# Two jobs of one unit moved ahead on TensorE: the GRU products to the second step, the sums over the table to the third, in a graph layer with a GRU update

## The reference

```python
h = relu(layernorm(x))
xs, xd = h[src], h[dst]
att = sigmoid(xs @ W_att[:d] + xd @ W_att[d:] + b_att)
messages = (xs @ W_msg + b_msg) * att
aggregated = segment_sum(messages, dst)
gi, gh = aggregated @ W_ih.T + b_ih, h @ W_hh.T + b_hh
r = sigmoid(i_r + h_r); z = sigmoid(i_z + h_z); n = tanh(i_n + r * h_n)
h_new = (1 - z) * n + z * h
out = x + gamma * (h_new - mean) * rsqrt(var + 1e-5) + beta
```

## Time and profile before

| what | value |
|---|---|
| median of 3 runs | 2257.42 us (2254.52 to 2258.43) |
| profiled execution, its own time | 2257.88 us |
| its span in the profile | 2256.1 us |
| busy share PE / DVE / ACT / POOL | 91% / 89% / 88% / 74% |
| mean granted clock of PE | 0.965 of full |

### The profile page before, as it was taken

One profiled execution on the slowest core, in us unless ns is written; L12 is line 12 of the kernel. 1 busy time (PEld: TensorE's weight loads), 2 busy tenths in 40 slices (PEclk: granted clock), 3 DMA queues, 4 the chain that ended last, 5 costly groups with the idle time before them and its releaser, 6 DMA issues.

```text
span 2256.1 us, 53903 instructions
## 1 busy us (share of the span) xinstructions
PE 2055.7 (91%) x18202; PEld 1994.3 (88%) x18202; DVE 2012.9 (89%) x4413; ACT 1996.3 (88%) x6980; POOL 1660.4 (74%) x1578
## 2 busy tenths in 40 slices
PE   3536999999999999999999999999999999999997
PEld 3525999999999999999999999999999999999996
DVE  5967899999999999999999999999999999999974
ACT  1368999999999999999999999999999999999943
POOL 4575777777777777777777777777777777777760
PEclk8865999999999999999999999999999999999998
DMA  6862222222222222222222222222222222222236
GB/s 164 237 172 62 56 60 62 59 60 60 62 62 62 63 58 64 61 63 59 63 59 62 59 61 60 63 60 62 60 61 63 59 62 60 61 61 64 58 108 231
DMA packets 167473, 171.57 MB, mean 76 GB/s; under 512 B 79462, under 2 KB 131736, under 8 KB 166944
## 3 DMA queue, kind: packets, MB, share of 16 engines
q0 software_dynamic: 49856, 102.96, 20.3%
q1 hardware_dynamic: 114564, 61.63, 10.5%
q10 hardware_dynamic: 2776, 3.52, 0.7%
HBM read 141.32 MB, written 26.65 MB: 74 GB/s over the span
## 4 chain that ended last, share of the span: by engine, by line
ACT 53%; PE 23%; DVE 14%; issue 7%; DMA 2%; SPq 1%; POOL 0%; ACTq 0%; DVEq 0%
ACT big L901 41%; PE ps L1456 12%; ACT gate_ring L897 9%; DVE big L1200 4%; PE ps L1441 4%; PE ps L1451 3%; DVE gate_ring L1184 2%; DVE key_hot L1170 1%; PE ps L1462 1%; PE ps L1463 1%; DVE lo_hot L1163 1%; DMA big<-in_x_dram 1%; DVE big L1129 1%; DMA row_ring<-node_table,set_idx 1%; ACT n_blk L906 1%
## 5 line engine op out<-in xcount | busy, mean ns | idle before, releaser
L773 POOL DMA_INDIRECT row_ring<-node_table,set_idx x1480 | 1571.8, 1062 | 473.4 <-issue 334.5
L901 ACT ACTIVATE big<-set_score,big 128x128 f32<-128x128 f32 x5096 | 1633.2, 394 | 81.0 <-PE ps L1456 80.7
L1456 PE MATMUL ps<-big 128*128 128x128 f32 x10192 | 1447.4, 281 | 0.0
L1456 PEld LDWEIGHTS ps<-big 128*128 128x128 f32 x10192 | 1265.0, 193 | 0.0
L1200 DVE TENSOR_TENSOR big<-ps,big 128x784 f32<-128x784 f32 x832 | 802.0, 964 | 10.2 <-ACT big L901 5.4
L1441 PE MATMUL ps<-gate_ring,row_ring 128*128 128x64 f32 x2960 | 534.8, 263 | 78.0 <-DVE gate_ring L1184 72.7
L1441 PEld LDWEIGHTS ps<-gate_ring,row_ring 128*128 128x128 f32 x2960 | 454.0, 194 | 124.4 <-DVE gate_ring L1184 110.7
L1184 DVE SCALAR_TENSOR_TENSOR gate_ring<-lane,set_rel,gate_ring 128x64 f32<-128x64 f32 x1480 | 412.9, 279 | 140.1 <-ACT gate_ring L897 135.0
L897 ACT ACTIVATE gate_ring<-set_win,row_ring 128x64 f32<-128x64 f32 x1480 | 493.2, 341 | 30.5 <-DMA row_ring<-node_table,set_idx 27.3
L1451 PE MATMUL ps<-key_hot,lo_hot 128*128 128x196 bf16 x3328 | 425.8, 250 | 14.4 <-DVE key_hot L1170 9.5
L1170 DVE TENSOR_TENSOR key_hot<-lane_key,set_key 128x1568 bf16<-128x1568 bf16 x416 | 402.0, 966 | 0.0
(11 more groups left out here) (129 smaller groups left out, 917.2 us busy)
## 6 DMA issues: line engine op xcount, KB each, us to landing
row_ring<-node_table,set_idx POOLq DMA_INDIRECT x1480
big<-in_x_dram SPq DMA_DIRECT2D x48, 256.0 KB, 5.6
h_blk<-hT_spill SPq DMA_DIRECT2D x97, 64.0 KB
node_table<-big SPq DMA_DIRECT2D x24, 258.0 KB
hT_spill<-big SPq DMA_DIRECT2D x24, 256.0 KB, 4.8
out_dram<-big SPq DMA_DIRECT2D x24, 256.0 KB
set_win<-dst_scores SPq DMA_DIRECT2D x148, 32.0 KB
set_score<-dst_scores SPq DMA_DIRECT2D x52, 64.0 KB
```

Of the source, the lines that this page charges most:

```text
L773: nc.gpsimd.indirect_dma_start(row_ring[:, t % ROWS_RING, :], None, table, bass.IndirectOffsetOnAxis(ap=set_idx[:, t // SET % 2, t % SET:t ...
L901: return nc.scalar.activation(a_buf[b % 2][:, h, :], set_score[:, b % 2, :], ACT.Sigmoid, bias=m_all[:, h, D:ROW])
L1456: return nc.tensor.matmul(ps[:, AM_BANK, 0:P], m_all[:, h, 0:D], a_buf[b % 2][:, h, :], start=h == 0, stop=h == HI - 1)
```

## The change

Three things change, all on PE. The sums over the table start at step 2 instead of 3. The GRU products of the finished block stand in step 1 instead of 2. In step 2 the `build` comes behind the part of the sums and not ahead of it. No instruction is added or taken away, and no other engine's program differs.

```diff
-PARTS_AT = 3
+PARTS_AT = 2
 DENSE_AT = 7
 GROUP_LAG = 3
-GRU_AT = (2, 10, 18, 26, 33)
+GRU_AT = (1, 10, 18, 26, 33)
...
-                    if u < BLOCKS and s % PER_BEAT in (0, 2):
+                    builds = u < BLOCKS and s % PER_BEAT in (0, 2)
+                    if builds and s != PARTS_AT:
                         build(u, 2 * (s // PER_BEAT) + (s % PER_BEAT) // 2)
                     if u and s == PARTS_AT:
                         pe.wait_ge(pairs_kept, u * (2 * BEATS))
...
                         last.then_inc(block_parts, 1)
+                    if builds and s == PARTS_AT:
+                        build(u, 2 * (s // PER_BEAT) + (s % PER_BEAT) // 2)
                     k = job_at(u, s, GRU_AT)
```

## The result

| | before | changed |
|---|---|---|
| median of 12 runs each | 2258.29 us (2254.52 to 2261.99) | 2263.99 us (2261.38 to 2266.70) |
| span of the profiled execution | 2256.1 us | 2262.1 us |

The ratio is 1.0021, with a 95% interval of 1.0013 to 1.0028. The change makes the kernel slower by 0.2%, where 24 us less were forecast; the range ended at 2257.

What follows compares the result with a forecast made beforehand. The prediction took two equally long chains, POOL's gathers and the loop of ACT, DVE and PE, to bound the kernel. Its sum was 2257.9 − 21.5 − 2.2 − 0.7 = 2233.5 us, range 2206 to 2257.

Steps and rivals of the forecast that it cites:

- What bounds the kernel: Main loop: POOL's gathers, never idle, and the loop of ACT, DVE and PE run equally long, 38.62 us a unit.
- The loop's 1.17 us: Start of each unit: ACT's wait for the sums falls from 1.47 to 0.3 us, shortening the loop by 1.17.
- PE's idle time: Step 1 on PE: the GRU products fill the idle 0.75 us before the next tile, which is then gone.
- What 1.17 us is worth: POOL's gathers limit the gain: from 1.367 to 1.351 us each, −21.5 us over 1345 gathers.
- rival 2: POOL keeps 1.367 us a gather and the loop's gain turns into ACT's waits for gathers: 2255 us, chance 0.22.
- The ends: First units: POOL's stops at the ring may go, −2.2 us; last unit: part of the sums done earlier, −0.7.
- rival 3: Builders always meet gathers at a bad moment, POOL slower, from a mean of 1.372 on: 2289 us, chance 0.09.
- Rival 1: The loop alone bounds the kernel, POOL settling at 37.45 us a unit: 2199 us, up to 2210, chance 0.20.
- The Trainium skill: Its rule that `tensor_tensor` does not hinder gather descriptors would give POOL 1.25 us a gather in a shorter unit.

Runs made afterwards that it cites:

- e1: The kernel before with every eighth gather left out from tile 40 on: 2257.57 us, 0.9984 of the kernel before.
- e2: The changed kernel with every eighth gather left out from tile 40 on: 2222.46 us, 0.9831 of the kernel before.
- e7: The changed kernel with the key builder cut into two instructions of half the size: 2228.19 us, 0.9868 of the kernel before.
- e9: The kernel before, PE's old order, with the key builder cut into two instructions: 2255.26 us, 1.0000 of the kernel before.
- e10: e7 with ACT's first gates of a unit's first GRU job in step 9 instead of 8: 2212.53 us, 0.9809 of the kernel before.
- e5: The changed kernel without the key builder (L1170) from unit 1 on, old patterns in its place: 2199.28 us, one execution.
- e6: The changed kernel without the other builder (L1163) from unit 1 on, old patterns in its place: 2212.24 us, one execution.
- e3: The kernel before with only the GRU products moved to step 1, sums still from step 3: 2266.88 us, 1.0026 of the kernel before.

## Why the prediction was wrong

**What bounds the kernel** was right: two chains of equal length, one of them POOL's without a pause. e1, e2, e7 and e9 show both halves of it. That the change would shorten the loop was right too.

**The loop's 1.17 us.** ACT's wait for the sums went from 1.47 us a unit to 0.07 (3.2 us in 46 units). Worked out was 0.3. But the loop gains less than that: with fewer gathers the new order brings 35 us (e2 against e1), 0.70 a unit, where 58 were worked out for the loop alone. The step missed a wait: ACT's first GRU gates stand in step 8 and need DVE's last step of the job before, in step 5; ACT now reaches them too early. With fewer gathers this wait is 28.9 us in e2 (0.6 a unit), and where it is removed, in e10, the kernel gains 13 us more than e7, each against its own kernel before. In the kernel before it does not show in the main loop, presumably because the wait ahead of it hid it. The forecast did not hang on this size, since it had POOL set the time either way.

PE's idle time did not go either. Over the main loop PE waited before for the masks of gathered tiles by

```profile
PE ps L1441 <- DVE gate_ring L1184: 49.6, 84, 1.1
```

and it waits 47.0 us with the change (in the waits above). Of the 49.6, 38.3 stood ahead of the tile of step 2; of the 47.0, 24.0 stand ahead of that of step 1 and 10.1 ahead of that of step 17.

**What 1.17 us is worth: here it failed.** The step took 1.351 us a gather, the middle between 1.367 and the 1.335 of four units with a broken pattern. Measured: 1.371. Of the forecast −21.5 us came +6.0 over the same 1345 gathers. Those four units were picked because their pattern was broken, and that says little about the new pattern. DVE ran the key builder 8 times in two of them and 7 times in the other two, against 8 in a unit on average, so the number of builders explains little. They differ in how long the gathers are that meet it: 1068, 1108 and 1103 ns on average in the three fast ones, 1394 in the slow one, 1225 over all 46 units. That depends on the moment of the meeting, which nothing in the step could foretell, and it came out at 1244. The honest figure was the mean of all 46, and rival 2 with 2255 was worked out from it. That the builders are what makes gathers long was right (e5, e6). That their cost is per unit of work, and not per time, no run separates.

**The ends.** Gathers 40 to 134: −2.8 for the −2.2 forecast. After the last gather: −2.1 for −0.7.

**The rivals.** The result lies between rival 2, unchanged pitch, and rival 3, slower. The mechanism is rival 3's at a small size: ACT does follow right behind the gathers, and the builders meet them at worse moments. The pitch came out at 1.371, where rival 3 began to count from 1.372, and its 2289 was far too much. The medians differ by 5.7 us, and 6.0 come from the pitch in the one pair of profiles; the rest of the balance there (5.0 ahead of gather 10, −2.8 and −2.1) is partly the scatter between executions. Rival 1, the loop alone at 2199, is what the kernel goes towards when gathers are fewer or cheaper: 2222 in e2, 2228 in e7, both with POOL waiting for the ring.

**The Trainium skill.** By "SBUF — State Buffer", "Who interferes with whom", a `tensor_tensor` should not hold up the descriptors of a gather, which the page marks as inferred. The same section of the Trainium skill also says that a `tensor_tensor` with both inputs in SBUF contends with GpSimd's reads, which the prediction left out. e5 and e6 show that both builders, `tensor_tensor` on bf16 from SBUF to SBUF, make gathers longer: by 97 and 38 ns of the mean. The measurement decides: the inference does not hold for this pair, and it was no reason to count on rival 1. Whether it is a read of POOL that is held up, no run shows.

## What to carry to other kernels

Before a wait is removed, look for an engine that never idles even if its busy share is the lowest: POOL at 74% set the time of the changed kernel, and the 0.30 us between its gathers are neither counted as busy nor free. When two chains are equally long, a change of one is worth nothing and may look useless; test it with the other chain made artificially short (here every eighth gather left out) before it is dropped. And a mean for the time after a change comes from all units, not from those that happen to look like what one hopes for.

## What was not expected of the hardware

- DVE's `tensor_tensor` on bf16 lengthens indirect DMAs issued by POOL: the mean gather is 1066 ns with both builders and 969 without the larger. Two instructions of half the size hold them up less than one whole: with the new order the mean went from 1066 to 1025 ns for 558 ns twice instead of 967 once.
- How much it costs goes by the moment of the meeting: the same builders beside the same gathers gave 1.367, 1.371 and 1.375 us a gather (the kernel before, the changed one and e3), with only PE's order changed and POOL never idle.
- The sign of a change of 0.2 to 0.5% was not the same in all series. Where the kernel before takes 2606 and 2567 us the change is faster; where it takes 2258, it is slower.
